# Graph stage of a three-stage kernel: both affinities of a pair in one run, its first bias behind the outputs, and the row loads between storing the values and waiting for them

## The chip, the cores and the metric

One Trainium2 chip, one core. The metric is the device time of one execution of the whole program in microseconds, the median of several runs. A profiled execution gives the trace from which all rows below come.

## What is computed

Per batch row (32 of them, 128 tokens, 128 features) a conditioned transformer block (attention with 16 heads, then a feed-forward part), and behind it a graph attention layer. The change touches only the graph layer:

```python
vcq = jnp.concatenate([exp_v, q_exp], axis=-1)
self_feat = vcq @ W_self.T + b_self
output = self_feat
for d in range(2):
    A = adj_f if d == 0 else jnp.swapaxes(adj_f, 1, 2)
    A = A[:, :, :NONGT, :]                     # NONGT = 20
    cond = A.sum(-1)
    vb = A @ w_bias + b_bias
    output = output + _gat_attention(self_feat, cond, vb, Wq[d], bq[d], Wk[d], bk[d], Wout[d], bout[d])
return exp_v + jax.nn.relu(output)
```

`_gat_attention` forms queries of all 128 tokens and keys of the first 20, for 16 heads of 8 features; multiplies them (the affinities), masks and adds the label bias, takes a softmax over the 20 keys, and multiplies the weights by values (here already turned by `Wout`), plus `bout`.

## The kernel before, in words

The kernel is written by engine: each engine has its own program, and the order of the calls in its `body(s)` is the order on that engine. Engines wait for each other by semaphores. PE is TensorE, DVE VectorE, ACT ScalarE, POOL GpSimd, SP the queue of SyncE, which here only issues DMAs.

The graph stage works on pairs of batch rows (16 steps, s.n = 0 to 15; `par` is s.n modulo 2 and picks the buffer). `body(s)` runs several pairs in a pipeline: the softmax and outputs of pair s, the affinities of pair s+1, self features, keys, queries and values of pair s+2, and the turning of the input of pair s+3. In the names, `(s, 0)` and `(s, 1)` are the two batch rows of a pair.

On PE: `turn_w` transposes softmax weights (L2150), `self_features` (L2084), `affinity` multiplies queries by block-diagonal keys in two halves of 64 rows (L2137), `weights_v` multiplies turned weights by value blocks (L2167), `turn_self` transposes self features (L2091), `turn_x` the input (L2076), then `values`, `keys`, `queries` (L2099 to L2126). `affinity(s, b)` waits for the queries, for the block keys and until the scores that stood in its bank were read (`shifted`). `turn_self` waits for `self_saved`, which DVE gives in `save_self`.

On DVE: `add_bias` (L2329) adds mask and label bias to an affinity in PSUM, `row_max` (L2339), `shift_scores` (L2343), `save_self` (L2315), `invert_sums` (L2350) and `save_out` (L2355) divide the outputs by the weights' sums, and `split_selfT` (L2322) makes the low part of the self features, waiting for ACT's copies (L2228, L2229). ACT also takes the exponentials (L2260) and copies the turned weights to SBUF (L2266).

The value blocks go through DRAM: ACT leaves the values in `v_rows`, SP stores them to a diagonal image (`v_image`, L1961), waits until these stores have landed, and loads the blocks from it (`g_v_block`, L1966). `weights_v(s, 0)` waits for these loads. SP also loads inputs (`g_x_in`, L1969, and `g_q_row`, L1970), the residual (L1974), and stores the result (L1983). A DMA issued on SP waits for everything ahead of it in SP's program.

Of the kernel before, what the change touches and what calls it, by code (L numbers as in the profile page):

```python
# [7 lines left out]
PAIRS = B // 2  # L8
# [43 lines left out]
def zero_wait(eng, s, value):  # L52

    if not isinstance(value, int) or value > 0:
        eng.wait_ge(s, value)
# [1270 lines left out]
def step_from(s, k):  # L1326

    return Step(s.half + (s.par + k) // 2, (s.par + k) % 2)


def more(s, k):

    return not isinstance(s.n, int) or 0 <= s.n + k < PAIRS


def at(s, n):

    return isinstance(s.n, int) and s.n == n
# [440 lines left out]
def graph_phase(nc, g, ctx, edges):  # L1779
# [9 lines left out]
    def sem(name):  # L1789
        return ctx.enter_context(nc.semaphore(name))  # L1790
# [63 lines left out]
    self_full, self_saved = sem("g_self_full"), sem("g_self_saved")  # L1854
# [27 lines left out]
    def run_bodies(eng, body):  # L1882

        for n in range(4):
            body(Step(n // 2, n % 2))
        with eng.Fori(2, PAIRS // 2 - 2) as r:
            body(Step(r, 0))
            body(Step(r, 1))
        for n in range(PAIRS - 4, PAIRS + 1):
            body(Step(n // 2, n % 2))  # L1890

    def by_token(t):
        return t.rearrange("p (t b) -> p b t", b=2)
# [7 lines left out]
    def unit_count(s, b):  # L1901
        return s.n * 2 + (b + 1)
# [21 lines left out]
    def v_diagonal(n, b):  # L1924

        blocks = v_image[n, b].rearrange("(h x) -> h x", x=NG * ROW + GW)[:, 0:NG * ROW]
        return blocks.rearrange("h (m e) -> m h e", e=ROW)[:, :, 0:GW]
# [23 lines left out]
                sp.dma_start(v_windows(n)[b], v_part(n, b)).then_inc(v_image_cleared, 16)  # L1951

    def sync(sp):
        def move_values(s):

            if at(s, 0):
                sp.wait_ge(v_image_cleared, 4 * 16)
            zero_wait(sp, v_loaded[s.par], s.half * 32)
            sp.wait_ge(v_saved, s.n + 1)
            for b in range(2):  # L1960
                sp.dma_start(v_diagonal(s.par, b), v_rows[b:BM:2]).then_inc(v_stored[s.par], 16)  # L1961
            sp.wait_ge(v_stored[s.par], s.half * 32 + 32)

            zero_wait(sp, out_full, unit_count(step_from(s, -2), 1))
            for b in range(2):
                sp.dma_start(v_part(s.par, b), v_windows(s.par)[b]).then_inc(v_loaded[s.par], 16)  # L1966

        def load(s):
            sp.dma_start(x_in[:, s.par], g.x2_p[s.n]).then_inc(x_loaded[s.par], 16)  # L1969
            sp.dma_start(q_row[:, s.par],  # L1970
                         g.rows_p[s.n].partition_broadcast(128)).then_inc(q_row_loaded[s.par], 16)

        def load_res(s):
            sp.dma_start(x_res[:, s.par], g.x2_p[s.n]).then_inc(res_loaded[s.par], 16)  # L1974

        def store(s):
            if at(s, PAIRS - 1):
                for b in range(2):
                    sp.wait_ge(last_ready, b + 1)
                    sp.dma_start(g.out_p[s.n][:, b], y[:, s.par, b]).then_inc(y_stored[s.par], 16)  # L1980
                return
            sp.wait_ge(y_ready, s.n + 1)
            sp.dma_start(g.out_p[s.n], y[:, s.par]).then_inc(y_stored[s.par], 16)  # L1983

        def body(s):
            if more(s, 4):

                done = step_from(s, 2)
                sp.wait_ge(self_saved, done.n + 1)
                load(step_from(s, 4))  # L1990
            if more(s, -1):
                store(step_from(s, -1))
                if more(s, 1):

                    load_res(step_from(s, 1))
            if more(s, 2):
                move_values(step_from(s, 2))

        for n in range(2):
            sp.wait_ge(g.x2_stored[n], 16)  # L2000
            load(Step(0, n))
        for n in range(2):
            load_res(Step(0, n))
        sp.wait_ge(g.x2_stored[0], 2 * 16)
        body(Step(-1, 0))
        sp.wait_ge(g.x2_stored[1], 2 * 16)
        body(Step(-1, 1))
        for n in range(2):
            sp.wait_ge(g.x2_stored[n], PAIRS // 2 * 16)
        run_bodies(sp, body)  # L2010
        for n in range(2):
            sp.wait_ge(y_stored[n], (PAIRS // 2 + n) * 16)

# [53 lines left out]
    def tensor(pe, steps=False):  # L2067
# [20 lines left out]
        def turn_self(s):  # L2088
            pe.wait_ge(self_saved, s.n + 1)
            for b in range(2):  # L2090
                last = pe.transpose(by_token(turns_ps[:, 0:2 * T])[:, b], self_nat[:, s.par, b, :], g.ident[:])  # L2091
            last.then_inc(selfT_full, 1)
# [35 lines left out]
        def affinity(s, b):  # L2128
            if b == 0:
                pe.wait_ge(q_saved, s.n + 1)  # L2130
            pe.wait_ge(k_block_ready, unit_count(s, b))

            zero_wait(pe, shifted, unit_count(s, b) - 2)
            for d in range(2):
                for half in range(2):
                    rows = slice(64 * half, 64 * half + 64)
                    last = pe.matmul(aff_ps[b][:, half, d].rearrange("p h m -> p (h m)"), qT[rows, d, b, :],  # L2137
                                     k_block[rows, s.par, b, d].rearrange("p h m -> p (h m)"), start=True, stop=True)
            last.then_inc(aff_full, 1)
# [36 lines left out]
        def body(s):  # L2176
            here, nxt, second = more(s, 0), more(s, 1), more(s, 2)

            if at(s, PAIRS - 1):
                multiply_identity(turns_ps[:, 0:T], FILL + 2)  # L2180
            if here:
                turn_w(s, 0)
            if at(s, PAIRS - 1):
                multiply_identity(g.bank[0][:, 512:512 + T], FILL)
            if second:
                self_features(step_from(s, 2))
            if nxt:
                affinity(step_from(s, 1), 0)
            if here:
                weights_v(s, 0)  # L2190
            if second:
                turn_self(step_from(s, 2))

            if here:
                turn_w(s, 1)
            if at(s, PAIRS - 1):
                multiply_identity(g.bank[0][:, 512:512 + T], FILL)
            if nxt:
                affinity(step_from(s, 1), 1)
            if more(s, 3):  # L2200
                turn_x(step_from(s, 3))
            if second:
                values(step_from(s, 2))
                keys(step_from(s, 2))
                queries(step_from(s, 2))
            if here:
                weights_v(s, 1)
# [92 lines left out]
    def vector(dve, test_last_rows=None, steps=False):  # L2300
# [25 lines left out]
        def add_bias(s, b):  # L2326
            dve.wait_ge(aff_full, unit_count(s, b))
            for half in range(2):
                last = dve.tensor_tensor(aff_ps[b][:, half], aff_ps[b][:, half],  # L2329
                                         g.sums[:, :, bias_at(s, b)].unsqueeze(2)  # L2330
                                         .broadcast_to([128, 2, HALF, NG]), ALU.add)
            last.then_inc(biased, 1)
# [19 lines left out]
        def save_out(s, b):  # L2352
            dve.wait_ge(r_sum_ready, unit_count(s, b))

            dve.tensor_tensor(o[:, s.par, b].rearrange("p d (h v) -> p d h v", h=GH), out_ps[:, :, :, 0:GD],  # L2355
                              r_sum[:, b].unsqueeze(3).broadcast_to([128, 2, GH, GD]),
                              ALU.mult).then_inc(o_ready, 1)
# [21 lines left out]
        def body(s):  # L2379
            here, nxt, second = more(s, 0), more(s, 1), more(s, 2)  # L2380

            if here:
                add_bias(s, 1)
                row_max(s, 1)
            if more(s, -1):
                invert_sums(step_from(s, -1), 1)
                save_out(step_from(s, -1), 1)
            if at(s, PAIRS):
                finish_last(step_from(s, -1), 1)
            if here:  # L2390
                shift_scores(s, 1)
            if at(s, 0):
                test_last_rows()
            if second:
                save_self(step_from(s, 2))

            if nxt:
                add_bias(step_from(s, 1), 0)
            if here:
                invert_sums(s, 0)  # L2400
                save_out(s, 0)
            if at(s, PAIRS - 1):
                save_last_wT(s)
                finish_last(s, 0)
            if second:
                split_selfT(step_from(s, 2))
            if nxt:
                row_max(step_from(s, 1), 0)
                shift_scores(step_from(s, 1), 0)
# [156 lines left out]
```

## Time and profile before

| what | value |
|---|---|
| median of 3 runs | 590.4 us (588.36 to 593.13) |
| profiled execution | 590.79 us, span 589.2 us |
| PE, PE weight loads busy | 98%, 90% of the span |
| DVE, ACT, POOL busy | 86%, 79%, 50% |
| granted clock of PE, mean | 0.994 |

Shares of busy time are means over the three stages. Matmuls are pipelined and overlap in the rows, so a start is a surer mark than a length; an instruction on DVE also starts a little before the end of the one ahead if it doesn't need its result.

### The profile page before, as it was taken

Reading aid. Unit: us, or ns where it says so; the run is one execution under the profiler, and the core shown is the slowest. Engines: PE = TensorE matmul, PEld = TensorE weight load, DVE = VectorE, ACT = ScalarE, POOL = GpSimd, SP = SyncE. Lnnn points to the kernel's source line nnn. Section 1 sums busy time; section 2 is a strip of 40 time slices with the busy share of each in tenths; the row PEclk is TensorE's granted clock in tenths of the full one; section 3 lists DMA queues with packets and bytes.
Section 4 is the critical chain, followed back from the end, with each engine's and each line's share of the span. In section 5 each row is a group of like instructions: output and inputs, shape, how many; then the busy total and the mean of one; then the engine's idle time right before and its main releaser. Section 6 shows DMA issues by size and latency. Waiting matters only on the chain.

```text
span 589.2 us, 17159 instructions
## 1 busy us (share of the span) xinstructions
PE 574.6 (98%) x5504; PEld 528.5 (90%) x5504; DVE 508.5 (86%) x1112; ACT 467.3 (79%) x1654; POOL 293.9 (50%) x355
## 2 busy tenths in 40 slices
PE   8999799999999999999999999999999999999987
PEld 8899699999999999999999999988988899998876
DVE  5899888998889889988888899888785999998976
ACT  4988589879897898898888978977886777776753
POOL 4547345354354453543553635555664455655642
PEclk9999899999999999999999999999999999999989
DMA  8210201202102102021021041113352565545642
GB/s 254 77 42 8 53 20 42 58 0 57 45 12 57 35 22 57 6 52 49 9 57 39 18 106 30 42 55 100 107 149 78 112 129 124 107 100 118 128 94 62
DMA packets 99095, 39.92 MB, mean 68 GB/s; under 512 B 59617, under 2 KB 96881, under 8 KB 99057
## 3 DMA queue, kind: packets, MB, share of 16 engines
q1 hardware_dynamic: 97280, 35.21, 25.5%
q0 software_dynamic: 1632, 4.21, 2.4%
q8 instruction: 21, 0.34, 0.3%
q14 instruction: 18, 0.14, 0.1%
q10 hardware_dynamic: 144, 0.02, 0.0%
HBM read 31.64 MB, written 7.78 MB: 67 GB/s over the span
## 4 chain that ended last, share of the span: by engine, by line
PE 71%; DMA 9%; SPq 8%; DVE 7%; issue 3%; ACT 2%; POOL 0%; DVEq 0%; ACTq 0%; POOLq 0%
PE banks L724 10%; PE banks L754 9%; PE banks L737 9%; DMA v_image<-g_v_rows 8%; PE banks L692 5%; PE banks L693 5%; PE banks L696 5%; PE banks L1527 4%; PE banks L777 2%; PE banks L779 2%; PE banks L778 2%; PE banks L708 2%; PE banks L710 2%; PE banks L709 2%; SPq L1966 2%
## 5 line engine op out<-in xcount | busy, mean ns | idle before, releaser
L611 POOL TENSOR_TENSOR late_blocks<-late_blocks,p_rsum 128x512 f32<-128x512 f32 x96 | 99.0, 1052 | 159.9 <-DVE p_rsum L1101 159.8
L951 ACT ACTIVATE late_blocks<-banks,neg_max 128x128 f32<-128x128 f32 x384 | 137.2, 405 | 28.0 <-DVE neg_max L1095 28.0
L951 ACT ACTIVATION_READ_ACCUMULATOR late_blocks<-banks,neg_max 128x1 f32 x384 | 94.3, 246 | 0.0
L1095 DVE TENSOR_REDUCE neg_max<-banks 128x8 f32<-128x1024 f32 x64 | 76.5, 1196 | 3.2 <-PE banks L724 3.2
L932 ACT ACTIVATE wide<-banks 128x512 f32<-128x512 f32 x124 | 75.6, 611 | 4.6 <-PE banks L696 1.6
L692 PE MATMUL banks<-xT_hi,w_qkv_hi 128*128 128x256 f32 x256 | 77.8, 304 | 0.0
L693 PE MATMUL banks<-xT_lo,w_qkv_hi 128*128 128x256 f32 x256 | 72.4, 283 | 0.0
L696 PE MATMUL banks<-xT_hi,w_qkv_lo 128*128 128x256 f32 x256 | 72.2, 282 | 0.0
L724 PE MATMUL banks<-wide 64*128 64x128 f32 x1024 | 66.6, 280 | 0.2
L724 PEld LDWEIGHTS banks<-wide 64*128 64x128 f32 x1024 | 60.3, 189 | 6.3 <-issue 3.9
L951 ACT ACTIVATE third_p<-banks,neg_max 128x128 f32<-128x128 f32 x128 | 46.9, 387 | 23.7 <-DVE neg_max L1095 23.7
L1119 DVE CAST oT_hi<-banks 128x512 fp32r<-128x512 f32 x62 | 42.3, 683 | 10.8 <-PE banks L754 10.6
L737 PE MATMUL banks<-ident,late_blocks 128*128 128x128 f32 x384 | 50.7, 275 | 0.9 <-DVE x L1152 0.6
L692 PEld LDWEIGHTS banks<-xT_hi,w_qkv_hi 128*128 128x128 f32 x256 | 48.5, 190 | 1.0
L693 PEld LDWEIGHTS banks<-xT_lo,w_qkv_hi 128*128 128x128 f32 x256 | 48.7, 190 | 0.6
L696 PEld LDWEIGHTS banks<-xT_hi,w_qkv_lo 128*128 128x128 f32 x256 | 48.4, 189 | 0.0
L2021 POOL TENSOR_TENSOR late_blocks<-blockmask,g_kT 128x320 f32<-128x320 f32 x32 | 27.2, 870 | 41.1 <-ACT g_kT L2249 41.1
L737 PEld LDWEIGHTS banks<-ident,late_blocks 128*128 128x128 f32 x384 | 42.8, 140 | 5.3 <-issue 0.8
L1124 DVE TENSOR_TENSOR oT_lo<-banks,oT_hi 128x512 fp32r<-128x512 f32 x64 | 43.9, 686 | 2.3 <-ACT oT_hi L1030 1.2
L2167 PEld LDWEIGHTS banks<-g_v_block,g_wT 128*128 128x128 f32 x320 | 40.3, 193 | 5.5 <-DMA g_v_block<-v_image 2.7
L2167 PE MATMUL banks<-g_v_block,g_wT 128*128 128x63 f32 (+2 forms) x320 | 43.1, 282 | 2.2 <-DMA g_v_block<-v_image 1.5
L754 PE MATMUL banks<-second_pT,v 128*64 128x128 f32 x512 | 34.3, 277 | 3.1 <-DVE v L1158 3.1
(186 smaller groups left out, 1676.9 us busy)
## 6 DMA issues: line engine op xcount, KB each, us to landing
g_v_block<-v_image SPq DMA_DIRECT2D x32, 180.0 KB, 2.9
early<-in_mask SPq DMA_DIRECT2D x16, 220.0 KB
early<-in_mask SPq DMA_DIRECT2D x80, 44.0 KB
x_in<-in_x SPq DMA_DIRECT2D x16, 128.0 KB, 2.2
x_res<-in_x SPq DMA_DIRECT2D x16, 128.0 KB, 2.2
x_scratch<-x SPq DMA_DIRECT2D x16, 128.0 KB, 1.9
f_x_in<-x_scratch SPq DMA_DIRECT2D x16, 128.0 KB, 2.5
f_x_res<-x_scratch POOLq DMA_DIRECT2D x16, 128.0 KB, 2.7
```

The lines of the kernel that those rows point to most:

```text
L611: pool.tensor_tensor(p[:, heads, :], p[:, heads, :], p_rsum[:, b, heads].unsqueeze(2).broadcast_to([128, 4, T]), ALU.mult).then_inc(p_read ...
L692: pe.matmul(dst, g.wq_hi[:, cols], xT_hi[par][:], start=True, stop=False)
L693: pe.matmul(dst, g.wq_hi[:, cols], xT_lo[par][:], start=False, stop=False)
L696: last = pe.matmul(dst, g.wq_lo[:, cols], xT_hi[par][:], start=False, stop=True)
L724: last = pe.matmul(s_ps[b][:, e, j, :], qk[rows, c, 0, b, :], qk[rows, c, 1, b, :], start=True, stop=True)
L737: last = pe.transpose(work_ps[bank][:, m * T:m * T + T], p[:, 4 * grp + m, :], g.ident[:])
L754: last = pe.matmul(work_ps[bank][64 * e:64 * e + 64, j * T:j * T + T], v[:, b, head * DH:head * DH + DH], pT[b][:, 2 * j + e, :], start=Tr ...
L932: act.activation(qk_dst(name) if name[0] == "q" else v_dst(name), work_ps[bank], ACT.Copy).then_inc(bank_free[bank], 1)
L951: act.activation(p[:, m, :], s_ps[b][:, e, j, :], ACT.Exp, bias=neg_max[:, b, 4 * e + j:4 * e + j + 1], accum_out=p_sum[:, b, m:m + 1]).th ...
L1095: dve.tensor_reduce(out=neg_max[:, b, :].rearrange("p (e j) -> p e j", e=2), in_=s_ps[b], op=ALU.max, axis=AX.X, negate=True).then_inc(max ...
L1124: dve.tensor_tensor(oT_lo[:, 4 * half:4 * half + 4, b, :], src, oT_hi[:, 4 * half:4 * half + 4, b, :].bitcast(F32), ALU.subtract).then_inc ...
L2167: last = pe.matmul(outputs[:, begin:end], wT[:, c, :], v_block[:, s.par, b, c, begin + AHEAD - BASE * c:end + AHEAD - BASE * c], start=(c ...
```

## The change

On SP, the step `move_values` is cut in two, `store_values` and `load_values`, and the load of input and query row (now for the pair five ahead of the body, `load_behind`) is put between them. The wait of that load is for `self_saved` of two pairs before the loaded one, as it was. The first and last rounds are written out, and the loop is a turn shorter. On PE, both calls of `affinity` stand together behind `turn_self` and ahead of the second `turn_w`. On DVE, the first `add_bias` stands behind `invert_sums` and `save_out` of the first batch row. The lines of the changed kernel are shifted by 17 and more.

```diff
+        def load_values(s):
             sp.wait_ge(v_stored[s.par], s.half * 32 + 32)
             zero_wait(sp, out_full, unit_count(step_from(s, -2), 1))
             for b in range(2):
                 sp.dma_start(v_part(s.par, b), v_windows(s.par)[b]).then_inc(v_loaded[s.par], 16)
...
+        def load_behind(s):
+            done = step_from(s, -2)
+            sp.wait_ge(self_saved, done.n + 1)
+            load(s)
+
         def body(s):
-            if more(s, 4):
-
-                done = step_from(s, 2)
-                sp.wait_ge(self_saved, done.n + 1)
-                load(step_from(s, 4))
             if more(s, -1):
                 store(step_from(s, -1))
                 if more(s, 1):
 
                     load_res(step_from(s, 1))
             if more(s, 2):
-                move_values(step_from(s, 2))
+                store_values(step_from(s, 2))
+            if more(s, 5):
+                load_behind(step_from(s, 5))
+            if more(s, 2):
+                load_values(step_from(s, 2))
...
             if second:
                 self_features(step_from(s, 2))
-            if nxt:
-                affinity(step_from(s, 1), 0)
             if here:
                 weights_v(s, 0)
             if second:
                 turn_self(step_from(s, 2))
+            if nxt:
+                affinity(step_from(s, 1), 0)
+                affinity(step_from(s, 1), 1)
 
             if here:
                 turn_w(s, 1)
             if at(s, PAIRS - 1):
                 multiply_identity(g.bank[0][:, 512:512 + T], FILL)
-            if nxt:
-                affinity(step_from(s, 1), 1)
...
-            if nxt:
-                add_bias(step_from(s, 1), 0)
             if here:
                 invert_sums(s, 0)
                 save_out(s, 0)
+            if nxt:
+                add_bias(step_from(s, 1), 0)
```

PE in one step of the written-out part, from the turned weights of the first batch row to `turn_x`. First before, then changed.

```order
L2150 MATMUL banks<-ident,late_weights 128x128 x5
L2084 MATMUL banks<-w_self_sb,g_xT 128x128 x2
L2137 MATMUL banks<-late_blocks,g_qT 128x160 x4
L2167 MATMUL banks<-g_v_block,g_wT 128x144
...
L2091 MATMUL banks<-ident,g_self 128x128 x2
L2150 MATMUL banks<-ident,late_weights 128x128 x5
L2137 MATMUL banks<-late_blocks,g_qT 128x160 x4
L2076 MATMUL banks<-ident,g_x_in 128x128 x2
```

```order
L2168 MATMUL banks<-ident,late_weights 128x128 x5
L2102 MATMUL banks<-w_self_sb,g_xT 128x128 x2
L2185 MATMUL banks<-g_v_block,g_wT 128x144
...
L2109 MATMUL banks<-ident,g_self 128x128 x2
L2155 MATMUL banks<-late_blocks,g_qT 128x160 x8
L2168 MATMUL banks<-ident,late_weights 128x128 x5
L2094 MATMUL banks<-ident,g_x_in 128x128 x2
```

The affinity of the next pair's first batch row moved behind `weights_v` and `turn_self`, that of the second one ahead of the second turning of weights.

DVE in one step, from the shifted scores of the second batch row to those of the next pair's first. First before, then changed.

```order
L2343 TENSOR_TENSOR late_weights<-banks,g_w_max 128x2x2x160
L2315 SCALAR_TENSOR_TENSOR g_self<-g_q_row,nonzero_rows,banks 128x128 x2
L2329 TENSOR_TENSOR banks<-banks,edge_sums 128x320 x2
L2350 RECIPROCAL g_r_sum<-banks 128x32
L2355 TENSOR_TENSOR late_outputs<-banks,g_r_sum 128x256
L2322 SCALAR_TENSOR_TENSOR g_selfT_lo<-banks,b_selfT_sb,g_selfT_hi 128x256
L2339 TENSOR_REDUCE g_w_max<-banks 128x32
```

```order
L2360 TENSOR_TENSOR late_weights<-banks,g_w_max 128x2x2x160
L2332 SCALAR_TENSOR_TENSOR g_self<-g_q_row,nonzero_rows,banks 128x128 x2
L2367 RECIPROCAL g_r_sum<-banks 128x32
L2372 TENSOR_TENSOR late_outputs<-banks,g_r_sum 128x256
L2346 TENSOR_TENSOR banks<-banks,edge_sums 128x320 x2
L2339 SCALAR_TENSOR_TENSOR g_selfT_lo<-banks,b_selfT_sb,g_selfT_hi 128x256
L2356 TENSOR_REDUCE g_w_max<-banks 128x32
```

The bias (`banks<-banks,edge_sums`) moved behind the reciprocal and the outputs; nothing else did.

SP in one round. First before, then changed.

```order
L1969 DMA g_x_in<-x_scratch 128x2x128
L1970 DMA g_q_row<-rows_scratch 128x256
L1983 DMA out<-g_y 128x2x128
L1974 DMA g_x_res<-x_scratch 128x2x128
L1961 DMA v_image<-g_v_rows 20x32x9 x2
L1966 DMA g_v_block<-v_image 128x5x72 x2
```

```order
L1985 DMA out<-g_y 128x2x128
L1976 DMA g_x_res<-x_scratch 128x2x128
L1961 DMA v_image<-g_v_rows 20x32x9 x2
L1971 DMA g_x_in<-x_scratch 128x2x128
L1972 DMA g_q_row<-rows_scratch 128x256
L1968 DMA g_v_block<-v_image 128x5x72 x2
```

The two row loads moved from the head of the round to between the value stores and the value loads.

## Rows read from the trace of the kernel before

**Rows 1.** Timeline of DVE over one step: start us, length us, engine, line, operation.

```profile
507.82 0.42 DVE L2355 TENSOR_TENSOR late_outputs<-banks,g_r_sum 128x256 f32<-128x256 f32 x1
508.16 0.81 DVE L2343 TENSOR_TENSOR late_weights<-banks,g_w_max 128x640 f32<-128x640 f32 x1
508.89 0.60 DVE L2315 SCALAR_TENSOR_TENSOR g_self<-g_q_row,nonzero_rows,banks 128x128 f32<-128x128 f32 x2
509.40 0.89 DVE L2329 TENSOR_TENSOR banks<-banks,edge_sums 128x320 f32<-128x320 f32 x2
510.46 0.36 DVE L2350 RECIPROCAL g_r_sum<-banks 128x32 f32<-128x32 f32 x1 [0.17 <-PE banks L2167]
510.85 0.42 DVE L2355 TENSOR_TENSOR late_outputs<-banks,g_r_sum 128x256 f32<-128x256 f32 x1
511.38 0.48 DVE L2322 SCALAR_TENSOR_TENSOR g_selfT_lo<-banks,b_selfT_sb,g_selfT_hi 128x256 fp32r<-128x256 f32 x1
...
513.37 0.89 DVE L2329 TENSOR_TENSOR banks<-banks,edge_sums 128x320 f32<-128x320 f32 x2
...
515.80 0.81 DVE L2343 TENSOR_TENSOR late_weights<-banks,g_w_max 128x640 f32<-128x640 f32 x1
```

**Rows 2.** Timeline of DVE, single rows of other steps.

```profile
463.50 0.59 DVE L2315 SCALAR_TENSOR_TENSOR g_self<-g_q_row,nonzero_rows,banks 128x128 f32<-128x128 f32 x2
...
464.82 0.34 DVE L2350 RECIPROCAL g_r_sum<-banks 128x32 f32<-128x32 f32 x1
...
469.95 0.81 DVE L2343 TENSOR_TENSOR late_weights<-banks,g_w_max 128x640 f32<-128x640 f32 x1
...
531.05 0.81 DVE L2343 TENSOR_TENSOR late_weights<-banks,g_w_max 128x640 f32<-128x640 f32 x1
...
563.03 0.81 DVE L2343 TENSOR_TENSOR late_weights<-banks,g_w_max 128x640 f32<-128x640 f32 x1
...
567.70 0.36 DVE L2350 RECIPROCAL g_r_sum<-banks 128x32 f32<-128x32 f32 x1 [2.54 <-PE banks L2167]
...
573.60 0.81 DVE L2343 TENSOR_TENSOR late_weights<-banks,g_w_max 128x640 f32<-128x640 f32 x1
```

**Rows 3.** Timeline of ACT, two places of the step of rows 1.

```profile
507.75 0.77 ACT L2266 ACTIVATE g_wT<-banks 128x384 f32<-128x384 f32 x2 [0.34 <-PE banks L2150]
...
511.06 0.29 ACT L2229 ACTIVATE g_kvT<-banks,b_selfT_sb 128x40 f32<-128x40 f32 x1
```

**Rows 4.** Timeline of SyncE's queue, one round.

```profile
499.31 1.60 SPq L1961 DMA_DIRECT2D v_image<-g_v_rows  x2
503.64 1.67 SPq L1966 DMA_DIRECT2D g_v_block<-v_image  x2
505.59 0.39 SPq L1969 DMA_DIRECT2D g_x_in<-x_scratch  x1
...
507.78 1.58 SPq L1961 DMA_DIRECT2D v_image<-g_v_rows  x2
```

**Rows 5.** Chain that ended last, near its end: start us, us, what.

```profile
560.86 4.70 DMA g_v_block<-v_image
```

**Rows 6.** The value loads (L1966) as a group.

```profile
DMA to landing us min/median/max: 2.5/2.9/4.7
```

**Rows 7.** Timeline of PE, in the first step and in that of rows 1.

```profile
464.15 0.44 PE L2091 MATMUL banks<-ident,g_self 128*128 128x128 f32 x2
...
507.77 0.61 PE L2084 MATMUL banks<-w_self_sb,g_xT 128*128 128x128 f32 x4
508.31 0.81 PE L2137 MATMUL banks<-late_blocks,g_qT 64*128 64x160 f32 x8
509.05 1.37 PE L2167 MATMUL banks<-g_v_block,g_wT 128*128 128x144 f32 x10
```

**Rows 8.** Timeline of PE, values' products in the step before the last.

```profile
576.67 1.37 PE L2167 MATMUL banks<-g_v_block,g_wT 128*128 128x144 f32 x10
```

**Rows 9.** Waits, 462 to 589 us: total us, times, longest us.

```profile
PEld banks L2137 <- issue: 3.2, 17, 0.3
```

More of the change, by code:

```diff
@@ L1953, in sync, with store_values @@
     def sync(sp):
-        def move_values(s):
+        def store_values(s):
             if at(s, 0):
@@ L1996, in body @@
             if more(s, 2):
-                move_values(step_from(s, 2))
+                store_values(step_from(s, 2))
[3 more added lines that the diff above has]
+                load_values(step_from(s, 2))
+        first, second = Step(0, 0), Step(0, 1)
         for n in range(2):
@@ L2004, in sync @@
         sp.wait_ge(g.x2_stored[0], 2 * 16)
-        body(Step(-1, 0))
+        load_behind(Step(1, 0))
+        store_values(first)
         sp.wait_ge(g.x2_stored[1], 2 * 16)
-        body(Step(-1, 1))
+        load_behind(Step(1, 1))
+        load_values(first)
+        store_values(second)
         for n in range(2):
             sp.wait_ge(g.x2_stored[n], PAIRS // 2 * 16)
-        run_bodies(sp, body)
+        load_behind(Step(2, 0))
+        load_values(second)
+        for n in range(4):
+            body(Step(n // 2, n % 2))
+        with sp.Fori(2, PAIRS // 2 - 3) as r:
+            body(Step(r, 0))
+            body(Step(r, 1))
+        for n in range(PAIRS - 6, PAIRS + 1):
+            body(Step(n // 2, n % 2))
         for n in range(2):
```

## The prediction, made before the changed kernel was run

> **What bounds the kernel now.** The last stage, the graph stage, runs from about 461 to 589 us of the span, one step for each pair of batch rows. I read the chain that ended last first, then the timeline of one step on each engine, and then compared the steps with each other.
>
> The step is set by VectorE (DVE). I time each step from the start of its second `shift_scores` (L2343), and call that moment T. Consecutive T lie 7.64 us apart (508.16 and 515.80 in [rows 1]; from 469.95 to 531.05 eight steps take 61.10 us, 7.64 each [rows 2]). Inside the step DVE waits only twice. It ends `add_bias` at 510.29 and starts `invert_sums` at 510.46, 0.17 us, released by the matmuls of `weights_v`. The second has no entry of its own and shows in the starts: where nothing is waited for, the next instruction starts 0.34 us after `save_out` (507.82 to 508.16), since its end overlaps what follows. Here `split_selfT` starts 0.53 us after `save_out` (510.85 to 511.38 [rows 1]), just as ACT ends the copy that it waits for (511.06 + 0.29 = 511.35 [rows 3]). That is 0.19 us. So 0.36 us of the 7.64 is waiting and 7.28 is work.
>
> Over that lies a second, slower clock: SyncE's queue. One round of it, from one store of the values to the next, takes 8.47 us (499.31 to 507.78 [rows 4]), more than a step. It starts with slack, falls behind by up to 0.8 us a round, and from step 9 on the others wait for it. From 531.05 to 563.03 four steps take 31.98 us where 4 x 7.64 = 30.56 would do: 1.42 lost. The next one takes 10.57 us (563.03 to 573.60), 2.93 too many, and there the chain of waits sits on the load of the value blocks for 4.70 us [rows 5], while DVE's row at 567.70 shows 2.54 us idle [rows 2]. Together the late queue costs 1.42 + 2.93 = 4.35 us in this execution.
>
> **The change, part by part.**
>
> *1. Rows loaded between storing and waiting (SyncE).* No DMA is added or removed. In a round of before the value stores start at 499.31 and the value loads at 503.64: 4.33 us, of which the queue issues for 1.60 and waits for 2.73 [rows 4]. The four other DMAs of the round take from 505.59 to 507.78, 2.19 us; half of it, 1.1 us, is the two loads `x_in` and `q_row`. They move into the wait. Queued behind them now are the value loads. The loads wait for `self_saved` of the step after, which comes 0.73 + 0.60 = 1.33 us after that step's T (508.89 + 0.60 = 509.49 [rows 1]). The value loads follow at about T + 1.33 + 1.1 = T + 2.5. The latest they may land is the start of `weights_v` in the next step, T + 7.83 + 0.1 (below). With 0.9 us for the second issue and the median landing of 2.9 us they land at T + 6.3; with the longest landing of the trace, 4.7 us [rows 6], at T + 8.1. The median has 1.6 us of room, the worst case is 0.2 late. The round itself shrinks from 8.47 to about 7.4 us and is shorter than the step. I take the whole 4.35 us as gained; the low end of the gain is 3.4, with one or two late landings left; a loss is the third rival.
>
> *2. Both affinities behind `turn_self` (PE), and the first bias behind the outputs (DVE).* The work on both engines is the same; only waits change. I follow DVE from T of a step.
>
> Before, `add_bias` fills DVE right behind `save_self`, since its affinity was multiplied long ago. Now `invert_sums` stands there, at T + 1.24 (509.40 - 508.16 [rows 1]). `weights_v` can start when `self_features` is through the array and the transposed weights are copied: ACT's two copies start at 507.75, 0.77 us for both, so the first is done near T + 0.07 [rows 3], and the last `save_out` at 507.82 + 0.42, T + 0.08 [rows 1]. Say T + 0.13 with the signal. In before it started at 509.05 and released DVE at 510.46, 1.41 later [rows 1, 7]. So `invert_sums` starts at T + 1.54: a wait of 0.30 in place of 0.17.
>
> `turn_self` needs `self_saved`, T + 1.33, plus 0.06 for the signal (463.50 + 0.59 = 464.09 on DVE against 464.15 on PE [rows 2, 7]): T + 1.39. Its two transposes take 0.44 where they start on an idle array [rows 7]. The affinity is issued 0.07 before the modelled end of what precedes it (507.77 + 0.61 = 508.38 against 508.31 [rows 7]): T + 1.76. It takes 0.81, and DVE starts 0.04 after the modelled end of a matmul (509.05 + 1.37 = 510.42 against 510.46). So `add_bias` can start at T + 2.61, while DVE is free from `save_out` at T + 1.54 + 0.39 + 0.34 = T + 2.27. That is a new wait of 0.34 us. It is the important one: it is a path DVE, PE, DVE that no later work can shorten.
>
> From `add_bias` on: 0.80 to `split_selfT` (its 0.89 less the 0.09 by which such an instruction overlaps one that doesn't need its result, 0.60 against 0.51 at 508.89; the copy on ACT is done by then), 1.99 from there to the second `add_bias` (511.38 to 513.37), and 2.43 to the next T (513.37 to 515.80 [rows 1]). The sum is 5.22, and T + 2.61 + 5.22 = **7.83 us for a step**, 0.19 more than before. PE doesn't set it: `turn_x` waits for `split_selfT` as before, and the PE work behind that is the same as before, so that the next step's first product comes in the same place against T.
>
> Bounds: PE is busy or waits through all of it, and if `turn_self` were released earlier than I reckon, the step would fall towards the 7.28 of pure work less about 0.09 (the overlap behind `add_bias`), so -0.45 a step. If `weights_v` starts late by 0.2, `turn_self` is queued behind it and the step is 7.95. I take 0.19, since each of its pieces is a row.
>
> *3. The first step and the tail.* In the first step of before neither of the two waits is there (the row at 464.82 has none [rows 2]), so it loses 0.19 + 0.36 = 0.55. In the step before the last, PE has nothing to do between turning the second weights and multiplying them by the values: the affinity that stood there is now ahead. Before, `weights_v` stood at 576.67, T + 3.07 [rows 8]. After: `weights_v` of the first row from T + 0.13 to 1.23, two affinities at 0.74 each (the distance from 508.31 to 509.05 [rows 7]) to T + 2.7, about half of a group of transposes, 0.35, and ACT's larger copy, some 0.5 of the 0.77 for both [rows 3], with the signal T + 3.6 to 3.7. That is 0.6 late (an estimate), and the last step's matmuls follow on PE without slack.
>
> **Sum**, against the profiled execution's own 590.79 us (span 589.2, 1.6 around it; the median of the three runs is 590.4, so they stand within 0.1%): -4.35 (queue) + 0.55 (first step) + 13 x 0.19 = 2.5 (the thirteen steps behind it that still prepare a pair) + 0.6 (tail) = -0.7. **590.1 us.** The two halves nearly cancel.
>
> A rule of the Trainium skill speaks for a better outcome: "TensorEngine Tiling (Array Packing)", Key Properties, says that a change of tiling mode drains TensorE. The trace agrees in kind, with 0.19 us of idle before each affinity [rows 9].
>
> **Rivals.**
>
> *The waits on DVE do not come.* If `add_bias` finds its affinity ready, or the step stays at 7.64 for another reason, what is left is -4.35 and the tail's +0.6: 587.0 us. For it: only 0.34 us of one wait has to be off. Against: the path is measured piece by piece.
>
> *PE was the bound, and the change saves it two drains.* The affinities are products of 64 rows amid ones of 128; PE's weight loads idle 3.2 / 17 = 0.19 us before them [rows 9]. In one run of both, one entry and one exit fall away, up to 0.38 us a step, 14 x 0.38 = 5.3, so 590.8 - 4.35 - 5.3 = 581 us. For it: PE's queue is nearly without gaps. Against: DVE is 7.28 of 7.64 busy, and PE's savings turn into waiting for `save_self`. It is the mechanism of the rule above.
>
> *The value loads come late in every step (slower).* Behind 256 KB of rows, and held by `self_saved` of the following step, they could land after T + 7.93. It decides from a landing of 4.5 us behind the second issue; the trace has 4.7 once and 2.9 as the median. If the loads ahead add 0.9 us and the longest landing is the rule, each step waits 0.2 + 0.9 = 1.1: 13 x 1.1 = 14, so 590.1 + 14 = 604 us. In the mild form, half of the steps by 0.9, it is 596.
>
> *`weights_v` is late and pushes `turn_self`.* Step 8.0 to 8.1: 13 x 0.25 = 3.3 more, 593.4 us.
>
> **How the numbers follow.** 0.60 for the forecast (588.5 to 592), 0.15 for waits that don't come (587), 0.08 for PE (581), 0.09 for late value loads (596 to 604), 0.08 for the pushed `turn_self` (593.4). The range from 586.0 to 594.0 holds all but the third, the fourth and some of the noise: the three runs of before lie from 588.36 to 593.13, and their spread comes from the same late queue. A measurement of this kernel tells about 1% from no change, 5.9 us: faster than 584.5 only with the drains, 0.09; slower than 596.3 with most of the late loads, 0.07; within, 0.84.
>
> **What the profile would show.** Right: T every 7.8 us through all thirteen steps, with no step of 8 or 10; the bias's first row behind `save_out` after about 0.34 us idle, put down to the affinity on PE; the first `invert_sums` after 0.3; no wait of PE on the value blocks; SyncE's value stores following the copy of the values at once, and its round as long as the step. Wrong: an idle PE ahead of `weights_v` put down to the DMA of the value blocks, or T under 7.6 us apart, which would say that the path through `turn_self` is shorter than its rows or that PE was the bound.

## The result, and the profile after

| | median | range | runs |
|---|---|---|---|
| before | 589.83 us | 586.83 to 593.19 | 20 |
| changed | 591.58 us | 589.84 to 592.77 | 20 |

The ratio is 1.0027, with a 95% interval of 1.0014 to 1.0040: the change costs about 1.6 us (1.7 between the medians). Below, a difference from before in us is worked out from its ratio, too; two other kernels are compared by their medians. 1.6 us is far inside the 1% within which I called "no change", and inside the range; but the forecast was 0.7 us faster, and the interval excludes it. The profiled execution took 592.77 us (span 591.2).

First the summary of the chain that ended last, from the page of the changed kernel.

```profile
PE 85%; DVE 9%; ACT 2%; issue 2%; DMA 1%; DVEq 0%; POOL 0%; ACTq 0%; SPq 0%; POOLq 0%
```

SyncE's queue and the DMA engines, 17% of the chain in before's first profile, are all but gone from it. That alone proves little: in the second profile of before (below) the chain has 0% of them as well. Now the same stretch of DVE as in [rows 1], one step inside the loop, from the timeline of the changed kernel.

```profile
503.70 0.81 DVE L2360 TENSOR_TENSOR late_weights<-banks,g_w_max 128x640 f32<-128x640 f32 x1
504.43 0.60 DVE L2332 SCALAR_TENSOR_TENSOR g_self<-g_q_row,nonzero_rows,banks 128x128 f32<-128x128 f32 x2
505.32 0.36 DVE L2367 RECIPROCAL g_r_sum<-banks 128x32 f32<-128x32 f32 x1 [0.29 <-PE banks L2185]
505.71 0.42 DVE L2372 TENSOR_TENSOR late_outputs<-banks,g_r_sum 128x256 f32<-128x256 f32 x1
506.42 0.90 DVE L2346 TENSOR_TENSOR banks<-banks,edge_sums 128x320 f32<-128x320 f32 x2 [0.29 <-PE banks L2155]
507.22 0.48 DVE L2339 SCALAR_TENSOR_TENSOR g_selfT_lo<-banks,b_selfT_sb,g_selfT_hi 128x256 fp32r<-128x256 f32 x1
...
511.59 0.81 DVE L2360 TENSOR_TENSOR late_weights<-banks,g_w_max 128x640 f32<-128x640 f32 x1
```

Both forecast waits are there, 0.29 for the outputs and 0.29 for the affinity; the wait of `split_selfT` is gone (507.22 stands 0.80 behind the bias). The forecast's 0.30 and 0.34 counted from the moment when DVE could have started, 0.09 and 0.08 us before the end of the instruction ahead; in the profile's count, from that end, they are 0.21 and 0.26. The step is 511.59 - 503.70 = 7.89 us. These are the pieces of the chain that ended last in this step (start, length, what).

```profile
503.94 1.34 PE banks L2185 x10
505.28 0.24 PE banks L2109 x2
505.52 0.77 PE banks L2155 x8
506.29 0.03 issue
506.31 0.06 DVEq L2346
506.37 0.05 issue
506.42 0.90 DVE banks L2346 x2
507.32 0.39 DVE g_selfT_lo L2339
```

The outputs' product, the turned self features, the affinity, the bias on DVE and then the low part of the self features, on which `turn_x` waits. The chain comes to `turn_self` (L2109) along PE and not from `save_self` on DVE, which looks like a contradiction of the forecast. The weight loads tell which of the two held it.

```profile
505.08 0.20 PEld L2109 LDWEIGHTS banks<-ident,g_self 128*128 128x128 f32 x2
```

`save_self` ends at 504.43 + 0.60 = 505.03, and the load starts 0.05 us later; it starts at T + 1.38 in all thirteen steps behind the first. By the single records of the trace it stands 0.13 to 0.15 us behind the last weight load of the outputs' product, where in before, whose self features were long saved, it stands 0.06 behind. So `save_self` releases it, as forecast, but the product on PE is done only some 0.1 us earlier.

And the queue of SyncE, one round, against [rows 4].

```profile
501.24 1.59 SPq L1961 DMA_DIRECT2D v_image<-g_v_rows  x2
505.25 0.40 SPq L1971 DMA_DIRECT2D g_x_in<-x_scratch  x1
505.84 0.91 SPq L1972 DMA_DIRECT2D g_q_row<-rows_scratch  x1
506.96 0.94 SPq L1968 DMA_DIRECT2D g_v_block<-v_image  x2
...
509.17 1.58 SPq L1961 DMA_DIRECT2D v_image<-g_v_rows  x2
```

The round is 7.93 us, as long as the step and no longer behind it. (The other rounds take 7.83 to 8.02 us from the third to the thirteenth.) The price of the rows ahead of the value loads shows in the page's row of these loads, 3.6 us to landing instead of 2.9:

```profile
g_v_block<-v_image SPq DMA_DIRECT2D x32, 180.0 KB, 3.6
```

It costs next to nothing; PE's waits for these loads add up to one of 0.2 us. In the steps inside the loop, the second load of a pair lands 0.2 to 1.5 us before PE starts on the blocks. The times from one T (the second `shift_scores` of a step) to the next, worked out from DVE's starts, show the two kernels at one glance. The third line is the kernel of the first experiment below; `T0` is at 462.28, 463.94 and 462.52 us.

```
step          0-1  1-2  2-3  3-4  4-5  5-6  6-7  7-8  8-9  9-10 10-11 11-12 12-13 13-14 14-15  T0 to T15
before        7.67 7.66 7.65 7.65 7.65 7.60 7.64 7.61 7.64 8.32  7.94  7.60  8.12 10.57  6.57    117.89
changed       8.31 7.83 7.84 7.83 7.95 7.89 7.94 7.89 7.95 7.89  7.94  7.90  7.83  7.78  7.24    118.01
loads alone   7.67 7.65 7.65 7.65 7.65 7.60 7.64 7.61 7.64 7.60  7.64  7.60  7.64  7.60  6.38    113.22
```

Every step of the changed kernel is longer than that of the loads alone, evenly; before has the steps of the loads alone up to step 9, and of the next five the queue makes four late (8.32, 7.94, 8.12, 10.57). In this pair of profiles the two nearly cancel over the graph stage (118.01 against 117.89). Most of the 2.0 us between the spans, 1.66, lies ahead of T0, in code that both kernels share. From 50 to 100 us the granted clock is 0.93 in the changed kernel's profile and 0.97 in that of before; in a later profile of the same changed kernel it was 0.97 and T0 at 462.23. Two executions can thus differ by 1.7 us before the change comes into play. So a pair of profiles doesn't explain 1.6 us of medians. The experiments do.

### The profile page after: what moved, and what is told of

Its sections match the earlier page's. It is cut to its first block, busy times and chain, and to the rows that moved or that the text cites. A ratio compares the mean times of both kernels' runs of the same rounds, so it can differ in the third digit from the quotient of the medians.

```text
span 591.2 us, 17133 instructions
## 1 busy us (share of the span) xinstructions
PE 573.8 (97%) x5504; PEld 527.9 (89%) x5504; DVE 508.5 (86%) x1112; ACT 467.8 (79%) x1654; POOL 294.0 (50%) x355
## 4 chain that ended last, share of the span: by engine, by line
PE 85%; DVE 9%; ACT 2%; issue 2%; DMA 1%; DVEq 0%; POOL 0%; ACTq 0%; SPq 0%; POOLq 0%
PE banks L724 10%; PE banks L754 10%; PE banks L737 9%; PE banks L2185 6%; PE banks L692 5%; PE banks L693 5%; PE banks L696 5%; PE banks L1527 3%; PE banks L778 2%; PE banks L777 2%; PE banks L779 2%; DVE banks L2346 2%; PE banks L708 2%; PE banks L710 2%; PE banks L709 2%; PE banks L2155 2%
## 5 line engine op out<-in xcount | busy, mean ns | idle before, releaser
L724 PE MATMUL banks<-wide 64*128 64x128 f32 x1024 | 67.8, 283 | 0.2
L2185 PE MATMUL banks<-g_v_block,g_wT 128*128 128x63 f32 (+2 forms) x320 | 41.7, 277 | 1.1 <-DVE late_outputs L2372 0.6
L2283 ACT ACTIVATE g_wT<-banks 128x384 f32<-128x384 f32 (+1 forms) x63 | 24.2, 435 | 20.9 <-PE banks L2168 20.9
```

The costliest lines, as they stand in the source:

```text
L724: last = pe.matmul(s_ps[b][:, e, j, :], qk[rows, c, 0, b, :], qk[rows, c, 1, b, :], start=True, stop=True)
L2185: last = pe.matmul(outputs[:, begin:end], wT[:, c, :], v_block[:, s.par, b, c, begin + AHEAD - BASE * c:end + AHEAD - BASE * c], start=(c ...
```

## The experiments

Each comes with the kernel before on the same chip. Three more chips were used, where before had medians of 587.33, 587.36 and 589.50 us. The changed kernel stood at 591.46 on the second of them, and was not run on the other two. The medians are of 6 to 12 executions, except for three variants of the changed kernel with 2 each, where it is said.

### The two parts apart

The loads alone: the diff of `sync` as in the change, `tensor` and `vector` as before.

> The changed order on SyncE alone; TensorE and VectorE keep the order of before. Theory (the late queue costs 3 to 4.4 us, the new order of the affinities costs a turn-around in every step): the step stays at 7.60 to 7.65 us through all thirteen steps, with no step of 8 to 10.6 us, and the time is 3 to 4 us under before, 586 us. Rival (the value loads were not late because of the queue, but because of the DMA engines): the long steps stay, and the time is that of before, 589.8.

586.62 us, ratio 0.9982 (0.9967 to 0.9997), 1.1 us under before (0.2 to 1.9). The steps are the third line of the table: no late one. The mechanism is as expected, and the size isn't: 1.1 us, not 3 to 4.

The order alone: the diff of `tensor` and `vector` as in the change, `sync` as before.

> The changed order on TensorE and VectorE alone; SyncE's queue as before, with rounds of about 8.0 us. Theory (the turn-around costs 0.2 to 0.3 us a step and hides most of the late queue, since the step comes near the queue's round): steps of 7.83 outside the loop and 7.9 in it, one or two late value loads near the end, 591 to 593.5 us. Rival (the new order saves two drains of TensorE a step and costs nothing, what is lost comes from the row loads ahead of the value loads): below before, 587 or less.

591.45 us, ratio 1.0059 (1.0036 to 1.0081), 3.5 us over before. Steps of 7.83, in the loop 7.89 to 7.94, and not one late, where I had expected one or two: T0 to T15 is 118.00, within 0.01 or so that of the whole change. SyncE's rounds, from the seventh on of 7.4 to 8.0 us, fit into a step that is longer by 0.2 to 0.3 us. That is, beside the new order the new place of the loads is worth nothing, and the even steps of the changed kernel don't prove it. The order's price is there in every run: 118.0 - 113.22 = 4.8 us in the profiles, 591.45 - 586.62 = 4.8 between the medians. Before pays a part of that anyway, through its queue.

### How much the late queue costs

The kernel before, profiled again on the first of these chips, and once more on the third.

> The kernel before, unchanged, for the spread of its late queue: in its first profile the queue cost 4.35 us. Theory: the loss varies from run to run, since it hangs on landings of the value stores and loads; 2 to 4.5 us here. Rival: it is the same 4.3 in each run.

587.83 us. Its steps are 7.60 to 7.67 up to step 10, then 7.79, 7.61, 8.50 and 7.76; T0 to T15 is 114.41, so the queue cost 114.41 - 113.22 = 1.2 us, less than the 2 to 4.5 that I had expected.

> The kernel before, a third profile, for the spread of the late queue (4.7 and 1.2 us more from the first T to the last than with the loads alone). Theory: again another value between 1 and 5 us, and each long step has its value loads issued late by SyncE. Rival: one of the two values again.

589.88 us. From step 8 on 7.97, 8.03, 7.79, 8.61, 8.09, 7.84; T0 to T15 is 115.87, 2.6 us of queue. In this profile SyncE's round, from one value store to the next, is to be seen falling behind the steps:

```profile
533.70 1.58 SPq L1961 DMA_DIRECT2D v_image<-g_v_rows  x2
...
541.26 1.58 SPq L1961 DMA_DIRECT2D v_image<-g_v_rows  x2
...
549.54 1.59 SPq L1961 DMA_DIRECT2D v_image<-g_v_rows  x2
554.25 0.94 SPq L1966 DMA_DIRECT2D g_v_block<-v_image  x2
...
557.66 1.58 SPq L1961 DMA_DIRECT2D v_image<-g_v_rows  x2
```

Rounds of 7.56, 8.28 and 8.12; of the last, 4.71 pass between the start of the value stores and the value loads. The value loads behind the long steps of this profile start at T + 5.2 to T + 6.1, where those of the loads alone start at T + 2.3 to T + 3.7 (steps 1 to 11 of both profiles), and PE takes up the blocks as they land, 0.04 to 0.07 us behind in five cases of six.

The three profiles of before give 4.7, 1.2 and 2.6 us, and I had taken 4.35 from the first as the gain. [rows 5, 6] held a warning: behind the step of 10.57 stands a single load that took 4.70 us, the longest of 32, where the median is 2.9. These 1.8 us are a slow landing more than a late queue.

The loads alone, again, on the third chip:

> SyncE's new order alone, again. Theory: steps 7.60 to 7.65 again, and 1 to 3 us under the kernel before on the same chip. Rival (its gain was chance): no difference.

586.73 us, ratio 0.9948 (0.9926 to 0.9969): 3.1 us under before (2.8 between the medians). The kernel without the late queue has the same time on both chips, 586.62 and 586.73; before has 587.33 and 589.50. What differs is the queue's cost, 1.1 and 3.1 us. The spread says the same: on this chip 23 executions of before lie from 587.0 to 593.3, and 12 of the loads alone from 586.0 to 587.4. This kernel, one part of the change by itself, beats both before and the changed kernel.

The changed kernel again:

> The changed kernel again, beside the kernel before on this chip. Theory (the order costs 4.8 us in any run; the late queue that it hides costs before 1 to 4 us, more on one chip than on the other): between 0.5 and 4 us above before; and the sum of the steps within 0.3 us of that in its first profile. Rival (the queue costs before a fixed 3.2): 1.6 us above.

591.46 us, ratio 1.0071 (1.0048 to 1.0093), 4.2 us over before. Its steps repeat to 0.01 or so (T0 to T15 117.99). A hair over the 4 of my expectation; the interval, 2.8 to 5.5 us, rules out the rival's fixed 1.6. With the order's 4.8 this leaves 0.6 us for the queue on that chip, and 4.8 - 1.6 = 3.2 on the one of the result; both are inferred, since the loads alone were run on neither.

### Is it the path through the self features?

```diff
             if nxt:
+                multiply_identity(g.bank[0][:, 320:320 + T], 2 if second else 0)
                 affinity(step_from(s, 1), 0)
                 affinity(step_from(s, 1), 1)
```

> The changed kernel with two idle multiplications of the identity (0.23 us each on TensorE) added in each step between turning the self features and the affinities; nothing reads them. Theory (the path VectorE, TensorE, VectorE through the self features sets the step): the step grows by the whole 0.46, to 8.3 us, and the time by about 14 x 0.46 = 6.4 us. Rival (TensorE has slack there, the step is set by VectorE's work or by the DMA queue): the step grows by less than 0.1.

598.65 us (2 executions), 7.2 over the changed kernel on the same chip. The steps are 8.28, in the loop 8.34 to 8.39: 0.45 more each, the whole of what was put in. By the profiles, 6.3 of the 7.2 us lie between T0 and T15; the rest lies ahead of T0, in code that both share. Timeline of DVE in a step outside the loop:

```profile
472.66 0.60 DVE L2333 SCALAR_TENSOR_TENSOR g_self<-g_q_row,nonzero_rows,banks 128x128 f32<-128x128 f32 x2
473.54 0.36 DVE L2368 RECIPROCAL g_r_sum<-banks 128x32 f32<-128x32 f32 x1 [0.29 <-PE banks L2185]
473.94 0.42 DVE L2373 TENSOR_TENSOR late_outputs<-banks,g_r_sum 128x256 f32<-128x256 f32 x1
474.99 0.90 DVE L2347 TENSOR_TENSOR banks<-banks,edge_sums 128x320 f32<-128x320 f32 x2 [0.63 <-PE banks L2155]
```

The wait for the outputs stays 0.29; that for the affinity grows from 0.18 to 0.63. The multiplications stand behind `turn_self`, on a stretch that the path from `save_self` shares with PE's own order, so this run shows that the stretch sets the step and not by which way it is reached; that is read from the weight load above, which starts at T + 1.38 here too.

The same two multiplications beside the path, at the head of the second turning of weights:

```diff
                 zero_wait(pe, wT_saved[part], unit_count(s, b) - 1)
+                if part == 0 and b == 1 and more(s, 2):
+                    multiply_identity(wT_ps[0][:, 0:T], 2)
```

> The same two idle multiplications, placed behind the affinities at the head of the second turning of weights. Theory (the two drains that TensorE saves came out as idle time of about 0.5 us ahead of turning the next input, which nobody needs): step unchanged, 7.83 to 7.95, time within 0.7 us of the changed kernel, and the idle time ahead of turning the input all but gone. Rival (TensorE is the bound): 0.46 a step, 6.4 us.

594.96 us (2 executions), 3.5 over the changed kernel, of which 2.6 lie between T0 and T15 by the profiles; steps of 8.05 to 8.07 behind the first. This falls between the two. DVE's waits for the affinity are as in the changed kernel (0.18 and 0.29), so the path above is untouched, but a new one opened: on DVE a wait for the second row's outputs, 0.18 in many steps, and the chain as the profile prints it runs on PE alone, from one `weights_v` to the next. So half of what I called idle was needed. The printed chain hides ACT's part: ACT copies the turned weights before it copies the turned input, the keys wait for the former (0.13 us of idle before their weight load at 476.75), and the queries' weight load at 477.24 starts as the latter is done. In this kernel the two copies start at 476.14 and 476.80; in the changed one the queries find the turned input copied. The slack on PE ahead of turning the next input was about 0.25 us, not 0.5.

The bias left ahead of the outputs:

```diff
-            if here:
-                invert_sums(s, 0)
-                save_out(s, 0)
             if nxt:
                 add_bias(step_from(s, 1), 0)
+            if here:
+                invert_sums(s, 0)
+                save_out(s, 0)
```

> The changed kernel with the first bias left where it was on VectorE, ahead of the outputs. Theory: VectorE stands idle until the affinity is there, T + 2.62 to 2.72, with the outputs queued behind it, so that a step is 2.62 + 0.89 + 0.39 + 0.34 + 4.42 = 8.6 to 8.7 us, 0.75 more than in the changed kernel, 10 us in all. Rival (the wait is short and the place of the bias makes no difference): 7.9 us.

601.88 us (2 executions), 10.4 over the changed kernel. Steps of 8.55 and in the loop 8.61 to 8.66, as worked out from the rows:

```profile
471.68 0.81 DVE L2360 TENSOR_TENSOR late_weights<-banks,g_w_max 128x640 f32<-128x640 f32 x1
472.41 0.60 DVE L2332 SCALAR_TENSOR_TENSOR g_self<-g_q_row,nonzero_rows,banks 128x128 f32<-128x128 f32 x2
474.29 0.90 DVE L2346 TENSOR_TENSOR banks<-banks,edge_sums 128x320 f32<-128x320 f32 x2 [1.28 <-PE banks L2155]
```

474.29 - 471.68 = 2.61: the affinity is ready at T + 2.61, exactly the moment of the prediction, and it is so whether DVE has 0.73 us of other work before it or none. The bias's new place is what holds the order's price down to 0.2 us a step outside the loop, where it would be 0.9; that part of the change is not the loss.

### Only the second affinity moved

With the new `sync`; the first affinity and the first bias as before.

```diff
             if second:
                 turn_self(step_from(s, 2))
+            if nxt:
+                affinity(step_from(s, 1), 1)
 
             if here:
                 turn_w(s, 1)
...
-            if nxt:
-                affinity(step_from(s, 1), 1)
```

> SyncE's new order, and of the order on TensorE only the second affinity moved (behind the turned self features, ahead of the second turning of weights); the first affinity and the first bias stay where they are in the kernel before. Theory (only the first affinity behind the self features makes the turn-around): steps 7.60 to 7.65 as with the loads alone; in the step before the last the values' product isn't covered any more, 0.3 to 0.6 us; so 0 to 0.6 us above the loads alone. Rival (any affinity ahead of the second turned weights costs, through the exponentials or the copies behind it): steps of 7.8.

588.29 us, 1.6 over the loads alone on the same chip and ratio 0.9981 (0.9962 to 1.0000) to before. Steps of 7.70 or 7.71, T0 to T15 114.36. Neither was right: the turn-around is not there (DVE's waits are the old ones, 0.18 for the first outputs among them), but each step is 0.07 longer. DVE loses it ahead of `invert_sums` of the second row, which starts 0.83 us behind the start of `row_max` in place of 0.74 to 0.78 in before, as the outputs' product on PE ends; the chain as printed is all PE, as in the kernel with the multiplications beside the path. PE in a step of it:

```profile
504.28 0.39 PE L2109 MATMUL banks<-ident,g_self 128*128 128x128 f32 x2
504.60 0.81 PE L2155 MATMUL banks<-late_blocks,g_qT 64*128 64x160 f32 x8
505.35 0.76 PE L2168 MATMUL banks<-ident,late_weights 128*128 128x128 f32 x5
505.95 0.43 PE L2094 MATMUL banks<-ident,g_x_in 128*128 128x128 f32 x2
```

The second turning of weights is late by an affinity, and the copies behind it come late too. Here too the queries' weight load starts as ACT's copy of the turned input is done. The tail costs 0.2 in step 14-15 and another 0.4 behind T15. So the second affinity's move by itself costs 1.6 us, through PE and ACT; the 4.8 of the whole order need the first one's as well, which makes the turn-around (no run has the first one's move alone). The two need not add up, since in the whole order DVE's path covers PE's.

### The tenth of a microsecond in the loop

The changed kernel with `run_bodies` of PE and DVE replaced by `for n in range(PAIRS + 1): body(Step(n // 2, n % 2))`.

> The changed kernel with the graph stage's loops on TensorE and VectorE written out, seventeen bodies in a row. Theory (inside the loop the wait of the first bias for its affinity is 0.3 instead of 0.18 us, since the semaphore waits against a register's value are instructions of their own there): every step 7.83 us, the wait 0.18 everywhere, 0.6 to 0.9 us under the changed kernel. Rival (the 0.1 us come from DMA or from position in the run): steps 5 to 12 stay at 7.89 to 7.95.

590.93 us, ratio 1.0053 (1.0036 to 1.0071); the order alone had 591.45 on that chip. Steps 1 to 13 are all 7.83 or 7.84, T0 to T15 117.33, 0.68 less than in the changed kernel. The wait is the same in every step:

```profile
519.61 0.36 DVE L2368 RECIPROCAL g_r_sum<-banks 128x32 f32<-128x32 f32 x1 [0.29 <-PE banks L2185]
520.00 0.42 DVE L2373 TENSOR_TENSOR late_outputs<-banks,g_r_sum 128x256 f32<-128x256 f32 x1
520.60 0.90 DVE L2347 TENSOR_TENSOR banks<-banks,edge_sums 128x320 f32<-128x320 f32 x2 [0.18 <-PE banks L2155]
```

So the loop costs 0.1 us at this wait. In the changed kernel's chain, above, an instruction of DVE's own queue (0.06 us, between two gaps of 0.03 and 0.05) stands there between affinity and bias. I take it for the wait against a register's value, which the loop needs and the written-out code doesn't. It is shown that the loop makes the difference, and argued from that row that the separate instruction does.

## Why the prediction was wrong

- The sum was 2.3 us too low (-0.7 against +1.6). Half of it is the gain, half the price.
- **The queue's gain**, -4.35 in the sum, is the first term that failed, by its size. The mechanism held: no late step in the loads alone or in their repeat, and the value loads come somewhat later than reckoned, but in time: in steps 1 to 11 of the changed kernel they start at T + 2.3 to T + 3.3 (for T + 2.5), take 3.6 us for 2.9 (the third rival had 0.9 more), and the second one lands at T + 6.7 to T + 7.9 (for T + 6.3), against a need at T + 8.0 or later. But the profile of before that I had was one with a large loss, 1.8 us of it from one slow landing. By three profiles the loss is 4.7, 1.2 and 2.6 us; by the two runs of the loads alone 1.1 and 3.1; and in the first comparison 3.2, which is inferred. I had the hint in hand, and wrote that the spread of before's three runs came from the late queue, and still took the gain of one run as that of the median, because the whole run stood near the median.
- **The turn-around**, 7.83 us a step, was right: 7.83 in the steps outside the loop, with the affinity ready at T + 2.61 as summed from the rows. The single waits were less well reckoned. In the profile's count they are 0.29 for 0.21, and outside the loop 0.18 for 0.26: the outputs' product began 0.1 later than I had it (503.94 is T + 0.24, not T + 0.13), so DVE came to the second wait later; the end of that wait, not its length, sets the step.
- **"DVE waits only twice" and "PE doesn't set it"** were nearly right. A third wait hides in the starts, in before as in the changed kernel. In the steps outside the loop `invert_sums` of the second row starts 0.78 us behind the start of `row_max` and 0.02 behind the end of its product on PE; in every second step in the loop it is 0.74, and PE was done 0.05 before. So from `split_selfT` on, PE's order is up to 0.04 us longer than DVE's work. Hence the steps of 7.60 and 7.64 by turns, and hence the two kernels that put more on PE there are slower: 0.83 with the second affinity early, 0.90 to 1.01 with the multiplications beside the path.
- **The loop** was missing, the first part of the price that I did not have: I used rows of before in which this wait is hidden. Eight steps at 0.09 more are 0.7 us.
- **The first step** was 0.64 for 0.55. **The tail** was 7.24 - 6.38 = 0.86 for 0.6: besides the uncovered values' product (0.45 us of idle, as forecast) PE waits 0.60 for `late_outputs` ahead of the first one in that step.
- The order in all: 4.8 us for 3.65; by parts 0.64 + 3.29 + 0.86. With the measured 1.1 to 3.1 us for the queue instead of 4.35 the sum is +1.7 to +3.7, and the two comparisons gave +1.6 and +4.2, one just outside at each end. That the time fell inside the range and within 1% says little for the sum: each half was off by more than 1 us, and both are small against 590 us.
- **Rivals.** The waits on DVE came, both of them. PE's drains are saved, and it doesn't help: what is saved comes out as waiting. These are rows of the changed kernel's waits (total us, times, longest us):

```profile
PE banks L2094 <- DVE g_selfT_lo L2339: 3.6, 13, 0.3
PEld banks L2155 <- issue: 2.3, 14, 0.2
```

  Such rows leave out gaps under 0.15 us, so the forecast's 0.19 "before each affinity" [rows 9] was misread: it is the mean of the 17 gaps that are listed. By the single records, PE's weight loads idle in a step of before 0.12 us ahead of the first affinity, 0.17 behind it, 0.17 ahead of the second and 0.28 ahead of `turn_x`; in the changed kernel 0.17 ahead of the two affinities, 0.17 behind them, and now 0.17 ahead of `weights_v`, which waits for ACT's copy, and outside the loop 0.44 ahead of `turn_x`, which waits for DVE. Together that is 0.74 us before and 0.95 after. The late value loads didn't come. Nor did a `weights_v` that pushes `turn_self`, though it came within some 0.1 us.

## What to carry to other kernels

A wait that a queue causes by falling behind varies from run to run; size it as a mean over several profiles, or by the spread of the times, before it is set against a loss that is there in every step. An engine that is nearly always at work (DVE, 7.28 of 7.64 us here) can still lose by a new turn-around through another engine: before moving a producer behind something that the consumer itself has to release, sum the path from release to return and compare it with what the consumer has to do meanwhile. And where a change has two parts that cancel, try each alone: here one of them, the loads in the shadow of the wait, was worth keeping (0.9982 and 0.9948), and the other lost more than it gained.

## What the runs showed of the hardware

- The same wait on DVE left 0.29 us idle inside a loop and 0.18 with the loop written out, 0.1 us more. That the separate instruction for a register's value is the reason is argued, not shown. It was seen only where the wait is a real one; in before's loop, where the affinity was long ready, the steps are even shorter than outside it (7.62 on average against 7.65).
- Two loads of 128 KB issued just ahead of the two value loads of 180 KB made these land 0.7 us later: a median of 3.6 us from issue to landing in both runs of the loads alone and in the changed kernel, 2.9 in the order alone, 2.8 and 2.9 in the repeats of before.
- "TensorEngine Tiling (Array Packing)", Key Properties, of the Trainium skill says that a change of tiling mode drains TensorE. The traces agree in kind: 2.3 / 14 = 0.16 us idle before a run of 64-row products, once a step in place of twice. But a gap of the same size, 0.17 us, stands before `weights_v` of the changed kernel, where the mode stays and PE waits for ACT, so the gap by itself doesn't name its cause. The saved gaps did not shorten the step, since `turn_self` and `turn_x` waited for DVE.
